# Half of a unit's running sums read by ScalarE and added by GpSimd

## The reference

```
g    = (x - mean_g) / sqrt(var_g + 1e-5)          # per image and group of 2 channels
x1   = g.sum(axis=1); m = x1 != 0                  # sum over the 64 channels, per pixel
mean, var of g per channel over the pixels with m  # padded to the largest count of an image
out  = x + where(m, g / sqrt(var + 1e-3), g)       # one scale and bias per image and channel
```

## Time and profile before

| | us |
|---|---|
| median of three executions | 1302.96 |
| lowest and highest | 1302.6, 1304.79 |
| the profiled execution's own time | 1303.82 |
| its span, first to last instruction | 1302.1 |
| VectorE busy | 1125.3 |
| ScalarE busy | 612.3 |
| TensorE matmuls busy | 609.0 |
| GpSimd busy | 75.8 |

### The profile page before, as it was taken

How to read it: one execution, slowest core, us unless ns; L and a number is a source line. 1 busy time by engine, 2 the same in 40 slices (tenths; PEclk the granted TensorE clock), 3 DMA queues, 4 the chain that set the end, 5 groups by cost and what they waited for, 6 DMA issues and landing times.

```text
span 1302.1 us, 9328 instructions
## 1 busy us (share of the span) xinstructions
PE 609.0 (47%) x2370; PEld 234.6 (18%) x2370; DVE 1125.3 (86%) x2356; ACT 612.3 (47%) x578; POOL 75.8 (6%) x140
## 2 busy tenths in 40 slices
PE   0555444455533555335553345543455434553355
PEld 0122211112211122111221112211112111221112
DVE  7999999998889898898988889888898888988894
ACT  0554444554434554345543355433554335543355
POOL 0000000000000000000000000000000000000000
PEclk9877666777657776667776677666777667776677
DMA  9999999999999999999999999999999999999996
GB/s 380 415 421 421 421 421 421 420 422 420 421 420 421 421 421 421 421 420 422 420 421 419 420 413 420 417 416 416 420 411 406 407 413 414 409 407 413 408 419 273
DMA packets 135461, 537.49 MB, mean 413 GB/s; under 512 B 4336, under 2 KB 4336, under 8 KB 135408
## 3 DMA queue, kind: packets, MB, share of 16 engines
q1 hardware_dynamic: 69936, 276.83, 52.5%
q10 hardware_dynamic: 65472, 260.05, 48.6%
HBM read 268.44 MB, written 268.44 MB: 412 GB/s over the span
## 4 chain that ended last, share of the span: by engine, by line
DMA 57%; DVE 15%; PE 12%; ACT 11%; issue 3%; SPq 0%; ACTq 0%; DVEq 0%
DMA out_dram<-slots 39%; DMA slots<-in_x_dram 18%; ACT slots L296 11%; PE flush L355 9%; DVE stats L407 7%; DVE sums L420 2%; DVE spread L390 2%; PE small_ps L334 1%; PE small_ps L344 1%; DVE dev L464 1%; PE small_ps L345 1%; DVE sums L417 1%; DVE spread L438 0%; DVE dev L436 0%; DVE by_image L442 0%
## 5 line engine op out<-in xcount | busy, mean ns | idle before, releaser
L407 DVE BATCH_NORM_STATS2 stats<-slots 128x6 f32<-128x512 f32 x1024 | 649.7, 678 | 96.5 <-DMA slots<-in_x_dram 94.7
L296 ACT ACTIVATE slots<-slots,out_bias,out_scale 128x1024 f32<-128x1024 f32 x512 | 592.6, 1229 | 197.9 <-issue 122.1
L355 PE MATMUL flush<-slots,weights 128*64 128x512 f32 x2048 | 515.6, 668 | 0.0
L420 DVE SCALAR_TENSOR_TENSOR sums<-flush,group_bias,sums 128x512 f32<-128x512 f32 x480 | 346.8, 738 | 31.2 <-PE flush L355 23.9
L334 PE MATMUL small_ps<-stats,group_avg 128*128 128x64 f32 x64 | 22.0, 445 | 431.2 <-DVEq L432 431.2
L355 PEld LDWEIGHTS flush<-slots,weights 128*64 128x64 f32 x2048 | 156.5, 154 | 331.4 <-issue 330.9
L308 ACT ACTIVATE by_image<-by_image,eps 128x16 f32<-128x16 f32 x32 | 9.8, 307 | 316.3 <-DVE by_image L442 316.3
L284 POOL TENSOR_TENSOR weights<-pair_sum,group_rstd 128x256 f32<-128x256 f32 x124 | 72.1, 614 | 1160.9 <-DVE group_bias L455 1160.9
L334 PEld LDWEIGHTS small_ps<-stats,group_avg 128*128 128x128 f32 x64 | 16.1, 312 | 458.5 <-DVEq L432 429.5
L310 ACT ACTIVATE col<-small_ps,eps 128x1 f32<-128x1 f32 x32 | 8.4, 261 | 164.8 <-PE small_ps L345 164.8
L334 PE MATMUL small_ps<-spread,group_avg 128*128 128x64 f32 x64 | 22.0, 447 | 117.3 <-DVE spread L438 117.3
(11 more groups left out here) (44 smaller groups left out, 151.6 us busy)
## 6 DMA issues: line engine op xcount, KB each, us to landing
slots<-in_x_dram SPq DMA_DIRECT2D x127, 2048.0 KB, 16.2
out_dram<-slots ACTq DMA_DIRECT2D x124, 2048.0 KB, 34.6
out_dram<-slots SPq DMA_DIRECT2D x16, 512.0 KB, 5.0
slots<-in_x_dram SPq DMA_DIRECT2D x4, 512.0 KB, 13.0
```

What stands on the lines that cost most here:

```text
L296: nc.scalar.activation(out_in_ring(u, i), image_in_ring(u, i), ACT.Identity, bias=out_bias[:, u % 2, i:i + 1], scale=out_scale[:, u % 2, i ...
L355: nc.tensor.matmul(bank[k * ROWS:(k + 1) * ROWS, :], weights[:, i, :], image_in_ring(u, i)[:, k * BLK:(k + 1) * BLK], start=True, stop=Tru ...
L407: last = V.bn_stats(stats[:, u % 2, k * BLOCK_STATS:(k + 1) * BLOCK_STATS], source)
L420: V.scalar_tensor_tensor(out=sums[:, i, :], in0=bank, scalar=share, in1=sums[:, i, :], op0=ALU.add, op1=ALU.add).then_inc(added, 1)
```

## The change

Of a unit's sixteen additions VectorE keeps those of the even images (`by_dve`), placed before blocks 8, 10, 14, 16, 18 and 22. For an odd image (`by_pool`) ScalarE, just before it writes that image's output, reads the bank with the mean's share as bias (`take`): in unit 0 straight into `sums`, later into the one buffer `fresh`, which it takes again only when GpSimd has added the contents before. GpSimd adds `fresh` to `sums`, after the weights of the same unit and before those of the next. TensorE waits for a bank on `added` or `taken`, by the image. The last unit's comparisons stay on VectorE and wait for either adder. The diff, without its first line of context and the declarations of two semaphores:

```diff
+FRESH_BUFS = 1
...
-    ADDS_BEFORE = {8: (0, 1, 2, 3, 4), 10: (5,), 12: (6,), 14: (7,), 16: (8, 9, 10), 18: (11,), 20: (12,), 22: (13,), 24: (14, 15)}
+    by_dve = list(range(0, B, 2))
+    by_pool = list(range(1, B, 2))
+    ADDS_BEFORE = {8: by_dve[0:3], 10: by_dve[3:4], 14: by_dve[4:5], 16: by_dve[5:6], 18: by_dve[6:7], 22: by_dve[7:8]}
...
+        fresh = sb("fresh", [P, FRESH_BUFS, BLK])
         sums = sb("sums", [P, B, BLK])
...
         def added_with(u, i):
-            return u * B + sum_order(u).index(i) + 1
+            return u * len(by_dve) + (sum_order(u) if u == LAST else by_dve).index(i) + 1
+
+        def taken_with(u, i):
+            return u * len(by_pool) + by_pool.index(i) + 1
+
+        def wait_for_bank(engine, u, i):
+            if u == LAST or i in by_dve:
+                engine.wait_ge(added, added_with(u, i))
+            else:
+                engine.wait_ge(taken, taken_with(u, i))
...
 # GpSimd, after the weights of unit u
+                if 0 < u < LAST:
+                    for i in by_pool:
+                        n = taken_with(u - 1, i) - 1
+                        pool.wait_ge(taken, taken_with(u, i))
+                        if u > 1:
+                            pool.wait_ge(added_by_pool, taken_with(u - 2, i))
+                        into = sums[:, i, :]
+                        pool.tensor_tensor(into, fresh[:, n % FRESH_BUFS, :], into, ALU.add).then_inc(added_by_pool, 1)
...
 # ScalarE
+            def take(u, i):
+                if u == 0:
+                    into = sums[:, i, :]
+                else:
+                    n = taken_with(u - 1, i) - 1
+                    into = fresh[:, n % FRESH_BUFS, :]
+                    if n >= FRESH_BUFS:
+                        act.wait_ge(added_by_pool, n + 1 - FRESH_BUFS)
+                nc.scalar.activation(into, bank_of(u, i), ACT.Identity, bias=group_bias[:, u % 2, i:i + 1]).then_inc(taken, 1)
...
                     if u < LAST or i >= APART:
                         wait_for_sum(act, u, i)
+                    if u < LAST and i in by_pool:
+                        take(u, i)
                     put_out(u, i)
...
 # TensorE
                     if m >= FLUSH_BANKS:
-                        pe.wait_ge(added, m + 1 - FLUSH_BANKS)
+                        before = (m - FLUSH_BANKS) // B
+                        wait_for_bank(pe, before, sum_order(before)[(m - FLUSH_BANKS) % B])
...
 # VectorE, count(i) in the last unit
-                dve.wait_ge(added, added_with(LAST - 1, i))
+                if i in by_dve:
+                    dve.wait_ge(added, added_with(LAST - 1, i))
+                else:
+                    dve.wait_ge(added_by_pool, taken_with(LAST - 2, i))
...
-            dve.wait_ge(added, UNITS * B)
+            dve.wait_ge(added, LAST * len(by_dve) + B)
```

More of the change, by code:

```diff
@@ L151, in norm_conv_kernel @@
         added = sem("added")
+        taken = sem("taken")
+        added_by_pool = sem("added_by_pool")
         out_ready = sem("out_ready")
@@ L191, in wait_for_sum, with bank_of @@
             engine.wait_ge(image_summed, (u * B + sum_order(u).index(i) + 1) * BLOCKS)
+        def bank_of(u, i):
+            return flush[(u * B + sum_order(u).index(i)) % FLUSH_BANKS][:, :]
         def added_with(u, i):
-            return u * B + sum_order(u).index(i) + 1
+            return u * len(by_dve) + (sum_order(u) if u == LAST else by_dve).index(i) + 1
[6 more added lines that the diff above has]
+                engine.wait_ge(taken, taken_with(u, i))
         def wait_for_all_stores(engine):
@@ L411, in add_sums @@
             def add_sums(u, i):
-                bank, share = flush[(added_with(u, i) - 1) % FLUSH_BANKS][:, :], group_bias[:, u % 2, i:i + 1]
+                share = group_bias[:, u % 2, i:i + 1]
                 wait_for_sum(dve, u, i)
                 if u == 0:
-                    V.tensor_scalar(sums[:, i, :], bank, share, None, ALU.add).then_inc(added, 1)
+                    V.tensor_scalar(sums[:, i, :], bank_of(u, i), share, None, ALU.add).then_inc(added, 1)
                 else:
                     dve.wait_ge(added, added_with(u - 1, i))
-                    V.scalar_tensor_tensor(out=sums[:, i, :], in0=bank, scalar=share, in1=sums[:, i, :],
+                    V.scalar_tensor_tensor(out=sums[:, i, :], in0=bank_of(u, i), scalar=share, in1=sums[:, i, :],
                                            op0=ALU.add, op1=ALU.add).then_inc(added, 1)
@@ L497, in count @@
                 wait_for_sum(dve, LAST, i)
-                bank = flush[(added_with(LAST, i) - 1) % FLUSH_BANKS][:, :]
-                dve.wait_ge(added, added_with(LAST - 1, i))
-                V.scalar_tensor_tensor(out=not_zero[:, i, :], in0=bank, scalar=group_bias[:, LAST % 2, i:i + 1],
+                if i in by_dve:
+                    dve.wait_ge(added, added_with(LAST - 1, i))
+                else:
+                    dve.wait_ge(added_by_pool, taken_with(LAST - 2, i))
+                V.scalar_tensor_tensor(out=not_zero[:, i, :], in0=bank_of(LAST, i), scalar=group_bias[:, LAST % 2, i:i + 1],
                                        in1=sums[:, i, :], op0=ALU.subtract, op1=ALU.not_equal,
```

## The result

The changed kernel takes 1299.58 us in the median of six runs (1298.59 to 1300.34), the one before 1304.75 (1302.6 to 1306.22) beside it: ratio 0.9963, 95% interval 0.995 to 0.9976. The change makes the kernel 0.37% faster. No change was forecast (1303.0 us), so the forecast is wrong, though the time lies in its range. The gain is neither VectorE's relief nor the tail, as the experiments show: it comes from the number of VectorE's instructions. Of all executions reported here one stood apart, 2164.7 us in the first run with small additions, and it is left out of that run's ratio.

The account below looks back on a forecast made before the run. The prediction took one late DMA engine's share of the bytes to bound the kernel. All five terms were 0, so it forecast no change, 1303.0 us, range 1298.5 to 1308.

Parts of the forecast that it names:

- What bounds it: Whole kernel: one of sixteen DMA engines falls behind, paces the loads through late-landing stores and sets the end.
- the time of the kernel is the time of its share of the bytes: Late DMA engine: hardly ever stands still; 33.6 MB over 1302.1 us is 25.8 GB/s, near its 26 to 27 alone.
- VectorE: worth 0: Units 0 to 30: eight additions fewer each, 183 us less work in all, but loads still set the pace; 0 us.
- ScalarE and GpSimd: worth 0: Added reads (0.7 us) and additions (1.2 us) fit in slack; 0, up to 2 us lost if early store cover failed.
- The port of VectorE and GpSimd: Shared SBUF port: small steps may wait for GpSimd's additions; even all serial, 3.7 us later against 4.33 idle, so 0.
- TensorE: Its waits for banks freed by ScalarE or VectorE: banks come free early enough; worth 0.
- The tail: it gains nothing: Last unit: final stores begin at 1271 instead of 1275.2, but the late DMA engine still ends about 1301.6; gain 0.
- the tail is given back: Rival, end of kernel: the hole from 1270 to 1276 is latency, so 4.1 us come off: 1298.9 us; chance 8%.
- The forecast marks: Signs expected in the changed profile: engine busy times, read and addition times, DMA rates, store landings and the hole near the end.
- Last landing stays at about 1301.6: Sign at the kernel's end: the last store lands when it did before, though the hole at 1270 shrinks to some 2 us.

Follow-up runs that it names:

- small additions: The kernel before with the odd images' additions of units 1 to 30 cut to one column, same instructions; ratio 1.0001, and 1.0002 when run again for its profile.

## Why the prediction was wrong

*What bounds it.* Right up to its last step. One DMA engine is late, paces the loads and decides the end; the experiment with small additions shows it: stores issued 3.5 us earlier, the last landing unmoved. The failed step is "the time of the kernel is the time of its share of the bytes". The engine makes 25.8 GB/s over the span and 26.4, a sixteenth of the full rate, alone, and the prediction let this difference pass as "next to". It is 25 us of 1302, between the span and 537.49 MB at 421 GB/s. The engine isn't slow, as the prediction had it; it does more: some 23 blocks of VectorE's instructions, of the 33 packets of q14 that part 3 of the page has at "0.0%". A share of sixteen engines hides what sits on one.

*VectorE: worth 0.* This is the term that was mis-sized. By busy time it was worth 0, as the run with small additions measured (1.0002). By instructions it was worth 488 x 1.06/128 = 4.0 us: eight additions and eight waits a unit, which the diff takes off VectorE. Measured were 4.8 us by the ratio, interval 3.1 to 6.5. That the time lies in the range is luck: its lower part was there for the tail's gain. The diff's lines were costed by what their instructions do on their engine, not by what it takes to bring them there.

*ScalarE and GpSimd: worth 0.* Right. A read took 0.678 us (0.7 taken), an addition 1.275 us (1.2 taken), no wait of ScalarE's for GpSimd shows in its row, and the first store of unit 29 even went out at 1200.0 for 1202.3. That their 959 instructions more are free was not argued in the prediction. The runs with more instructions on these engines show them free, up to about 25 blocks for ScalarE and 15 for GpSimd; the reason that fits is that their blocks don't go through the late engine.

*The port of VectorE and GpSimd.* GpSimd's additions disturbed little: VectorE's additions took 739 ns beside them, 738 before, the block statistics 681 for 678. But "no run of before shows a collision" is wrong, for one with GpSimd's weights stands in both kernels. Two small steps that VectorE takes while GpSimd forms the weights, in the kernel before, and then in the run where GpSimd has 1280 instructions more and so the parts of the weights come further apart:

```profile
L464 DVE TENSOR_SCALAR dev<-dev,small_ps 128x64 f32<-128x64 f32 x32 | 14.7, 458 | 0.0
L390 DVE SCALAR_TENSOR_TENSOR spread<-dev 128x64 f32<-128x64 f32 x32 | 18.1, 567 | 1.1
...
L513 DVE TENSOR_SCALAR dev<-dev,small_ps 128x64 f32<-128x64 f32 x32 | 8.3, 258 | 0.0
L439 DVE SCALAR_TENSOR_TENSOR spread<-dev 128x64 f32<-128x64 f32 x32 | 7.8, 244 | 1.1
```

They fall from 458 and 567 ns to 258 and 244, and VectorE from 959.2 to 943.4 us. The kernel gains nothing clear of noise by it (0.9954 for 0.9963).

*TensorE.* Right: its waits for VectorE's banks didn't show, and VectorE waited 82.3 us in all for TensorE's sums, 23.9 before, in time that it had.

*The tail: it gains nothing.* Right. The last stores came even earlier than forecast (1268.0 for 1271), and the landing followed only as far as the late engine had gained over the whole run. The rival "the tail is given back" gave 1298.9 us and the run 1299.58: near, and by a cause that isn't there.

*The forecast marks.* VectorE 959 us (about 940), ScalarE 751.5 (785, for a read adds only 0.56 us to its busy time, the rest overlaps), store landings past 35 us (38.6), 25 GB/s alone at the end, a hole of some 2 us: seen. "Last landing stays at about 1301.6": it was 1298.1, and that is what pointed to the cause.

The Trainium skill, "Runtime: NRT & Kernel Launch", section "Instruction fetch mechanics", says that each engine's sequencer has its own DMA queue for instructions and that fetching is hidden behind issuing. The runs agree that it is hidden from the engine (with 1707 instructions more VectorE still stood 223.1 us for loads) and show that it is not hidden from a DMA engine that is the bound. It gives blocks of 256 instructions; TensorE's q8 agrees (2048 more instructions are eight packets more, 28 for 20), VectorE's 122 an added packet of 8 KB don't. Own queues can't be seen: the profile has VectorE's, ScalarE's and GpSimd's packets under the one name q14 (14, 30 and 10 more for 1707, 3840 and 1280 instructions), and only the times tell them apart.

## What to carry to other kernels

In a kernel bound by DMA, look for one DMA engine that is behind: the rate in the last microseconds near a sixteenth of the full one, and the time to landing growing through the run. Then instructions are transfers too, and a wait that another wait covers can cost time although no engine waits for it: count the instructions that a change adds to each engine, waits among them, and hoist or merge them first on the engine whose blocks go through the late one. A time to landing that absorbs every saving ahead of it says that the saving was made in the wrong place.

## What the runs showed of the hardware that was not expected

An instruction that only waits, and for something long fulfilled, costs this kernel its share of a block: 1.06/128 us, 8 ns, on VectorE, though its own time on the engine (50 ns with two waits in it) costs nothing. A block of VectorE's costs its DMA engine 0.97 us between two landings although the packet's own record is 0.31 us (8 KB); a block of ScalarE's costs 0.65 us on another DMA engine. Which of the sixteen engines carries which blocks can't be read from the profile; it is inferred from the times. Why the two costs differ and why either is more than its packet is open, as is why TensorE's blocks of 16 KB, recorded at 0.9 us each, make no engine late: 28 of them didn't (0.995).
